# Attention, value copies and unit outputs in another order, one query chunk in a second bank

## The chip, the cores and the metric

The kernel runs on one core of a Trainium2 chip. The metric is the device time of one execution in microseconds (us); the number compared is the median of several executions. TensorE is called PE here, VectorE DVE, ScalarE ACT, GpSimd POOL, as in the profile.

## The reference

The model is one block of four phases on x, 1024 tokens by 256 features, each phase added to x behind a layer norm: attention, a mixture-of-experts feed-forward network, a state-space mixer, and the same feed-forward network again. The change is in the attention alone:

```python
q = (x @ wq.T).reshape(b, t, 16, 128).transpose(0, 2, 1, 3)      # 16 heads of 128
k = (x @ wk.T).reshape(b, t, 4, 128).transpose(0, 2, 1, 3)       # 4 key/value heads, each for 4 query heads
v = (x @ wv.T).reshape(b, t, 4, 128).transpose(0, 2, 1, 3)
scores = einsum('bhtd,bhsd->bhts', q, k_full) / sqrt(128)
mask = (k <= q) & ((k < 4) | (k >= q - 31))                       # 4 sink keys and a window of 32
attn = masked softmax of scores in float32
x = x + einsum('bhts,bhsd->bhtd', attn, v_full).reshape(b, t, 2048) @ wo.T
```

## The kernel before, in words

**Numbers.** Most products work on a high and a low part of each float32 operand (`three`, line 164: high by high, high by low, low by high), so a result that feeds another product is written twice: ACT copies the high part out of PSUM, then DVE subtracts it from the same PSUM bank and writes the low part. The bank is free only when the low part is out.

**Tiles.** The attention goes over 4 groups g (a key/value head with its 4 query heads), and in each over NJ = 11 units j: the first has 128 tokens, the others 90 (the last overlaps the one in front). That makes NU = 44 units. A unit is scores (PE), mask and row maximum (DVE, `row_max`), exponentials with their sums (ACT, `exps`, 4 pieces of 128x128 in a first unit and 3 pieces of 120x66 in the others, each an activation and an accumulator read), reciprocal of the sums (DVE, `recip`), normalisation (POOL, `normalise`), transposes (PE, `p_transpose`), high and low parts of the transposed probabilities (`pT_hi` L598 on ACT, `pT_lo` L691 on DVE), product with the values (PE, `p_v`), and high and low parts of the output (`oT_hi` L607 on ACT, `oT_lo` L697 on DVE).

**The value stage.** Ahead of the main loop a loop over j (lines 472, 581 and 676 for PE, ACT and DVE) makes the values of the 11 units. PE alternates between banks 4 and 5: value product j waits until low part j - 2 is out (`s_vlo`). ACT makes the high part (L585), DVE the low part (L680). The first three units are started inside this loop: `FIRST_UNITS` puts the scores, maxima and exponentials of units 0, 1 and 2 at j = 5, 7 and 9, and on ACT and DVE they stand in front of the value copy of the same j; `RECIPS` puts the reciprocals of units 0 and 1 behind j = 6 and 8.

**The main loop** (lines 526, 609 and 706) has one step i for each unit and some behind the last, 50 in all (0 to 49). Each engine has a fixed order within a step and runs its own list; only semaphores tie them together. In step i:

- PE: scores(i), query chunks of the step, projection of an output tile, p_v(i - 4), p_transpose(i - 2).
- ACT: copies of the query chunks (`q_evac`, L566), pT_hi(i - 3), oT_hi(i - 5), exps(i), and the high part of a weight in some steps.
- DVE: row_max(i), recip(i - 1), pT_lo(i - 3), the residual add of the step's tile (`add`, L704), in the last group the layer-norm statistics of that tile (L207, L210), oT_lo(i - 5), and in steps 44 to 48 the first stages of the next phase.
- POOL: gathers of keys, normalise(i - 1), low parts of weights.

A query chunk is 6 matmuls into bank 6 (`queries`, line 438); ACT copies it to `qT`, and the next chunk waits for that copy. Chunks 0 to 3 are in the value stage, chunks 4, 5 and then 6 and 7 together in steps 2, 3 and 4; units whose tokens lie behind 512 (from unit 5 on) wait for all eight. A projection (`project`, line 515) is 12 matmuls into bank 7. It waits for the low part of the last unit that its tile needs, which is oT_lo(i - 6), of the step before, and for the add that empties bank 7. p_v(i - 4) writes the bank of unit i - 6 (banks 4 and 5 in turn), so it too waits for oT_lo(i - 6). Each of the 8 tiles of a group has its projection in the step that lies 6 behind the last unit it needs: in the last group these are steps 39, 41, 42, 44, 45, 47, 48 and 49.

**The seam.** The next phase's stages for the first half of the tokens are queued into the last steps: on DVE `veps0` (step 44, L214), `norm0` (step 45, four L227), `lo0` (46), `logits_copy0` (47), `split0` (48, two low parts of weights, L867), on POOL `rstd0` (L221), on PE `tr0` (step 46, transposes, L235), `logits0` (47), `logits_tr0` (48), and then products of the next phase.

The DVE order of a step before the change:

```python
if 0 <= i - LAG_P < NU:
    pT_lo(i - LAG_P)
if i in y_tile:
    add(y_tile[i])
    if y_tile[i] >= (KV - 1) * NT:
        early(phase, "stats", e, y_tile[i] % NT)
if 0 <= i - LAG_F < NU:
    oT_lo(i - LAG_F)
```

Of the kernel before, what the change touches and what calls it, by code (L numbers as in the profile page):

```python
# [26 lines left out]
ACT = mybir.ActivationFunctionType  # L27
# [7 lines left out]
HALF = T // 2  # L35
# [7 lines left out]
HEADS, KV, HD = 16, 4, 128  # L43
GROUP = HEADS // KV
SINK, WINDOW = 4, 32
QB, NB_Q = 30, 3
# [8 lines left out]
NJ = 1 + -(-(T - P) // QT_LEN)  # L55
# [45 lines left out]
def build(nc, ins, out, phases=4):  # L101
    ctx = ExitStack()
    with ctx:
# [51 lines left out]
        def bank(i):  # L155
            return PS[:, i, :]
# [7 lines left out]
        def three(e, dst, lhs, rhs, start, stop, **kw):  # L164

            for n, (a, b) in enumerate(TERMS):
                i = e.matmul(dst, lhs(a), rhs(b), start=start and n == 0,  # L167
                             stop=stop and n == len(TERMS) - 1, **kw)
            return i
# [93 lines left out]
        def early(phase, stage, e, *args):  # L263

            if stage in phase["next"]:
                phase["next"][stage](e, *args)


        def attention():
# [3 lines left out]
            wq_hl = at("wq_hl", [P, 2, 2, KB, HALF], F32R, A_W)  # L273
            raw = at("w_raw", [P, 4, 1024], F32, A_W + 16384)
            qT = at("qT", [P, T, GROUP], F32, A_Q)
# [15 lines left out]
            s_q, s_qt, s_mask = sem("q_mm"), sem("q_ev"), sem("masked")  # L291
# [7 lines left out]
            phase = {"next": {}}  # L299
            units = [(g, j) for g in range(KV) for j in range(NJ)]  # L300
            NU = len(units)
# [13 lines left out]

            LAG_T, LAG_P, LAG_O, LAG_F, LAG_Y = 2, 3, 4, 5, 6
            FIRST_UNITS = {NJ - 6: 0, NJ - 4: 1, NJ - 2: 2}
            RECIPS = {NJ - 5: 0, NJ - 3: 1}
            NF = len(FIRST_UNITS)
            q_chunk = {NF - 1 + i: [GROUP + i] for i in range(3)}  # L320
            q_chunk[NF + 1].append(2 * GROUP - 1)
# [84 lines left out]
            def pe(e):  # L406
# [31 lines left out]
                def queries(n):  # L438
                    g, h = n // (2 * GROUP), n % GROUP
                    half = n // GROUP % 2  # L440
                    e.wait_ge(s_wl, WQ[g])
                    if n:
                        e.wait_ge(s_qt, n)
                    for k in range(KB):
                        m = three(e, bank(6), lambda w: wq_hl[:, g % 2, w, k, h * HD:(h + 1) * HD],
                                  lambda w: xT[:, w, k, HALF * half:HALF * half + HALF], k == 0, k == KB - 1)
                    m.then_inc(s_q, 1)

# [66 lines left out]
                def project(n):  # L515
                    g, t = n // NT, n % NT
                    e.wait_ge(s_olo, g * NJ + last_unit[t] + 1)
                    e.wait_ge(s_wl, WO[g])
                    if n:
                        e.wait_ge(s_add, n)  # L520
                    for h in range(GROUP):
                        m = three(e, bank(7)[:, 0:D], lambda w: oT_hl[:, w, h, t * P:(t + 1) * P],
                                  lambda w: wo_hl[:, g % 2, w, h, :], h == 0, h == GROUP - 1)
                    m.then_inc(s_y, 1)
# [21 lines left out]
            def act(e):  # L546
                ln["hi"](e, 0)
                w_hi(e, 0)
                w_hi(e, 1)
                w_hi(e, 2)  # L550
                ln["hi"](e, 1)
                e.wait_ge(LN["hi"], 2 * KB)
                for k in range(KB):
                    gather(e, lambda o, i: e.activation(o, i, ACT.Copy), HI, k).then_inc(s_xg, 1)
                ln["ready"](e)
                for k in range(KB):
                    gather(e, lambda o, i: e.activation(o, i, ACT.Copy), LO, k).then_inc(s_xg, 1)

                def q_evac(n):
                    h, half, g = n % GROUP, n // GROUP % 2, n // (2 * GROUP)  # L560
                    e.wait_ge(s_q, n + 1)
                    if g and half == 0:
                        e.wait_ge(s_s, (g - 1) * NJ + 6)
                    if g and half == 1:
                        e.wait_ge(s_s, g * NJ)
                    e.activation(qT[:, HALF * half:HALF * half + HALF, h], bank(6), ACT.Copy,  # L566
                                 scale=float(HD) ** -0.5).then_inc(s_qt, 1)

                def exps(u):
                    e.wait_ge(s_max, u + 1)  # L570
                    if u >= 4:
                        e.wait_ge(s_rd, u - 3)
                    rows, parts, p = probs(u)
                    for n in range(parts):
                        m = e.activation(p[:, n, :], p[:, n, :], ACT.Exp, bias=NEGM[0:rows, u % 4, n:n + 1],  # L575
                                         accum_out=DEN[0:rows, u % 4, n:n + 1])
                    m.then_inc(s_exp, 1)

                w_hi(e, 3)
                w_hi(e, 4)  # L580
                for j in range(NJ):
                    if j in FIRST_UNITS:
                        exps(FIRST_UNITS[j])
                    e.wait_ge(s_v, j + 1)
                    e.activation(v_hl[0:NK[j], HI, j, :], bank(4 + j % 2)[0:NK[j], :], ACT.Copy).then_inc(s_vhi, 1)  # L585
                    if j < GROUP:
                        q_evac(j)
                e.wait_ge(s_par, 16)
                e.wait_ge(s_cf, 16)
                e.activation(gw_hl[:, GW_PARTS:], cf[:, 0:GW_PAD - GW_PARTS], ACT.Copy, scale=0.0)  # L590
                e.activation(gw_hl[:, 0:GW_PARTS // 2], par[:, PR_GW:PR_CS], ACT.Copy).then_inc(s_gwh, 1)

                def pT_hi(u):
                    n, nk = GROUP * QN[units[u][1]], NK[units[u][1]]
                    e.wait_ge(s_t, u + 1)
                    if u >= 2:
                        e.wait_ge(s_o, u - 1)
                    e.activation(pT_hl[0:nk, u % 2, HI, 0:n], bank(2 + u % 2)[0:nk, 0:n], ACT.Copy).then_inc(s_phi, 1)  # L598

                def oT_hi(u):  # L600
                    g, j = units[u]
                    e.wait_ge(s_o, u + 1)
                    if g:
                        e.wait_ge(s_y, (g - 1) * NT + min(NT, -(-(Q0[j] + QN[j]) // P)))
                    if j and Q0[j] < Q0[j - 1] + QN[j - 1]:
                        e.wait_ge(s_olo, u)
                    e.activation(out_view(oT_hl[:, HI], j), out_psum(u, j), ACT.Copy).then_inc(s_ohi, 1)  # L607

                for i in range(STEPS):
                    for n in q_chunk.get(i, ()):  # L610
                        q_evac(n)
                    if 0 <= i - LAG_P < NU:
                        pT_hi(i - LAG_P)
                    if 0 <= i - LAG_F < NU:
                        oT_hi(i - LAG_F)
                    if NF <= i < NU:
                        exps(i)
                    if i in w_step:
                        w_hi(e, w_step[i])
                    if i == NU + 2:  # L620
                        early(phase, "hi0", e)

            def dve(e):
# [64 lines left out]
                def pT_lo(u):  # L688
                    n, nk = GROUP * QN[units[u][1]], NK[units[u][1]]
                    e.wait_ge(s_phi, u + 1)  # L690
                    e.tensor_tensor(pT_hl[0:nk, u % 2, LO, 0:n], bank(2 + u % 2)[0:nk, 0:n],  # L691
                                    f32(pT_hl[0:nk, u % 2, HI, 0:n]), ALU.subtract).then_inc(s_plo, 1)

                def oT_lo(u):
                    g, j = units[u]
                    e.wait_ge(s_ohi, u + 1)
                    e.tensor_tensor(out_view(oT_hl[:, LO], j), out_psum(u, j), f32(out_view(oT_hl[:, HI], j)),  # L697
                                    ALU.subtract).then_inc(s_olo, 1)
# [7 lines left out]
                for i in range(STEPS):  # L706
                    if NF <= i < NU:
                        row_max(i)
                    if NF <= i < NU + 1:
                        recip(i - 1)  # L710
                    if 0 <= i - LAG_P < NU:
                        pT_lo(i - LAG_P)
                    if i in y_tile:
                        add(y_tile[i])
                        if y_tile[i] >= (KV - 1) * NT:
                            early(phase, "stats", e, y_tile[i] % NT)
                    if 0 <= i - LAG_F < NU:
                        oT_lo(i - LAG_F)
                    for step, stage in ((NU, "veps0"), (NU + 1, "norm0"), (NU + 2, "lo0"), (NU + 3, "logits_copy0"),
                                        (NU + 4, "split0")):  # L720
                        if i == step:
                            early(phase, stage, e)

# [1419 lines left out]
```

## Time and profile before

| | |
|---|---|
| median of 3 runs | 570.72 us (568.29 to 571.48) |
| profiled execution, its own time | 568.28 us |
| its span, first to last instruction | 566.5 us |
| PE busy (matmul / weight load) | 525.1 us (93%) / 441.1 us (78%) |
| DVE, ACT, POOL busy | 405.4, 307.6, 127.2 us |
| granted TensorE clock | 0.995 |

The attention takes roughly the first 214 us of the span: layer norm and keys until about 26 us, the value stage until about 52, the main loop until about 214, of which the part behind the last scores (steps 44 to 49) begins at about 197. A busy PE in the profile is not yet PE at its peak, since matmuls overlap and their ends are modelled. An idle time in brackets is that of the row's engine ahead of the row, with what ended it.

### The profile page before, as it was taken

The numbers are of one execution on the slowest core, as the hardware profiler recorded it, in microseconds if no ns is written. First come the engines' busy times: TensorE is split into PE (matmuls) and PEld (weight loads), VectorE is DVE, ScalarE is ACT, GpSimd is POOL, SyncE is SP. The second block draws the span as 40 slices with busy tenths as digits, with TensorE's granted clock in tenths as the row PEclk, the third lists the DMA queues.
The fourth block names the chain that finished last, engine by engine and source line by source line (L and its number), as shares of the span: only waits on it lengthen the run. The fifth ranks groups of instructions, "written<-read, shape, count | busy, mean of one in ns | idle before, by whom it ended". The sixth has DMA issues, their size and how long they took to land.

```text
span 566.5 us, 9078 instructions
## 1 busy us (share of the span) xinstructions
PE 525.1 (93%) x3047; PEld 441.1 (78%) x3049; DVE 405.4 (72%) x895; ACT 307.6 (54%) x758; POOL 127.2 (22%) x272
## 2 busy tenths in 40 slices
PE   6998899999999888799999999999899889999994
PEld 4777799998999877577887887757777668788883
DVE  6534565666566878799877888957876868877684
ACT  3655778688677742454342455888752244333341
POOL 2322324244243210000000004667542000000000
PEclk9999999999999999999999999999999999999998
DMA  7320100000004003000030000000000000000101
GB/s 264 109 75 1 38 2 2 2 1 1 2 2 144 2 1 135 1 1 1 0 131 0 1 2 0 1 1 1 2 0 2 1 0 2 0 2 0 38 1 38
DMA packets 5790, 14.25 MB, mean 25 GB/s; under 512 B 624, under 2 KB 2928, under 8 KB 5744
## 3 DMA queue, kind: packets, MB, share of 16 engines
q1 hardware_dynamic: 5744, 13.66, 6.9%
q8 instruction: 25, 0.41, 0.3%
q14 instruction: 21, 0.17, 0.1%
HBM read 12.61 MB, written 1.05 MB: 24 GB/s over the span
## 4 chain that ended last, share of the span: by engine, by line
PE 65%; DVE 19%; ACT 7%; issue 6%; POOL 1%; DMA 1%; DVEq 0%; ACTq 0%; POOLq 0%
PE psum L167 53%; PE psum L468 2%; DVE f_t L1203 2%; DVE f_um L1213 2%; DVE oT_hl L697 1%; PE psum L500 1%; PE psum L235 1%; DVE ln_stats L207 1%; DVE x_resid L704 1%; ACT qT L566 1%; PE psum L997 1%; ACT pT_hl L598 1%; DVE xT_hl L249 1%; ACT f_sil L1110 1%; PE psum L1611 1%
## 5 line engine op out<-in xcount | busy, mean ns | idle before, releaser
L167 PE MATMUL psum<-xT_hl,ffn_w_hl 128*128 128x512 f32 x312 | 78.1, 397 | 7.3 <-DVE f_t L1203 7.3
L167 PE MATMUL psum<-f_um,ffn_w_hl 128*128 128x512 f32 x288 | 72.1, 398 | 1.2 <-DVE f_um L1213 1.2
L167 PEld LDWEIGHTS psum<-xT_hl,ffn_w_hl 128*128 128x128 f32 x312 | 56.3, 188 | 19.6 <-issue 8.7
L167 PEld LDWEIGHTS psum<-f_um,ffn_w_hl 128*128 128x128 f32 x288 | 53.5, 188 | 14.3 <-DVE f_um L1213 2.1
L1203 DVE TENSOR_TENSOR f_t<-psum,f_sil 128x512 f32<-128x512 f32 (+1 forms) x48 | 33.2, 691 | 32.8 <-ACT f_sil L1110 32.2
L1110 ACT ACTIVATE f_sil<-psum 128x512 f32<-128x512 f32 (+1 forms) x48 | 28.3, 597 | 51.8 <-PE psum L167 51.8
L167 PE MATMUL psum<-wo_hl,oT_hl 128*128 128x256 f32 x384 | 50.9, 282 | 4.1 <-DVE oT_hl L697 4.0
L691 DVE TENSOR_TENSOR pT_hl<-psum,pT_hl 126x360 fp32r<-126x360 f32 (+1 forms) x44 | 23.6, 537 | 42.9 <-ACT pT_hl L598 42.9
L167 PE MATMUL psum<-xT_hl,wq_hl 128*128 128x512 f32 x192 | 52.3, 407 | 1.9 <-ACT qT L566 1.9
L167 PEld LDWEIGHTS psum<-wo_hl,oT_hl 128*128 128x128 f32 x384 | 47.7, 188 | 7.5 <-DVE oT_hl L697 5.8
L1131 ACT ACTIVATE f_ch_hl<-f_ch 128x512 fp32r<-128x512 f32 x48 | 30.1, 630 | 41.4 <-DVE f_ch L1260 41.3
L566 ACT ACTIVATE qT<-psum 128x512 f32<-128x512 f32 x32 | 35.0, 1094 | 31.3 <-PE psum L167 31.3
L575 ACT ACTIVATE probs<-probs,small 120x66 f32<-120x66 f32 x120 | 40.8, 348 | 7.8 <-DVE small L674 7.1
L167 PEld LDWEIGHTS psum<-xT_hl,wq_hl 128*128 128x128 f32 x192 | 33.8, 189 | 9.2 <-issue 3.4
L167 PE MATMUL psum<-f_ch_hl,ffn_w_hl 128*128 128x512 f32 x144 | 37.8, 398 | 1.4 <-DVE f_ch_hl L1272 1.4
L167 PEld LDWEIGHTS psum<-ffn_w_hl,f_mix_hl 128*128 128x128 f32 x288 | 36.9, 188 | 2.8 <-DVE x_resid L1294 0.8
L167 PE MATMUL psum<-ffn_w_hl,f_mix_hl 128*128 128x256 f32 x288 | 37.7, 280 | 0.0
L746 POOL TENSOR_TENSOR probs_wide<-probs,small 120x186 f32<-120x186 f32 x40 | 20.0, 500 | 69.6 <-DVE small L654 69.3
L1260 DVE TENSOR_TENSOR f_ch<-f_t,f_wb 128x512 f32<-128x512 f32 x48 | 33.2, 691 | 1.4
L221 POOL TENSOR_TENSOR ln_rstd<-ln_var_eps,minus_half 128x4 f32<-128x4 f32 x8 | 8.1, 1012 | 114.5 <-DVE ln_var_eps L214 114.5
L167 PEld LDWEIGHTS psum<-f_ch_hl,ffn_w_hl 128*128 128x128 f32 x144 | 26.6, 188 | 8.7 <-DVE f_ch_hl L1272 2.0
L167 PE MATMUL psum<-pT_hl,v_hl 126*128 126x360 f32 (+1 forms) x132 | 30.5, 339 | 1.1 <-DVE oT_hl L697 0.6
(238 smaller groups left out, 1128.6 us busy)
## 6 DMA issues: line engine op xcount, KB each, us to landing
w_raw<-in_wq SPq DMA_DIRECT2D x4, 512.0 KB, 3.9
w_raw<-in_wo SPq DMA_DIRECT2D x4, 512.0 KB, 3.3
ffn_w_raw<-in_ffn SPq DMA_DIRECT2D x3, 576.0 KB, 6.3
ffn_w_raw_far<-in_ffn SPq DMA_DIRECT2D x3, 576.0 KB, 5.1
ssd_w_raw<-in_ssd SPq DMA_DIRECT2D x3, 512.0 KB, 5.4
x_resid<-in_x SPq DMA_DIRECT2D x2, 512.0 KB, 4.6
out_x<-x_resid SPq DMA_DIRECT2D x4, 256.0 KB, 2.3
w_raw<-in_wk SPq DMA_DIRECT2D x1, 512.0 KB, 6.6
```

The source lines that it names most:

```text
L167: i = e.matmul(dst, lhs(a), rhs(b), start=start and n == 0, stop=stop and n == len(TERMS) - 1, **kw)
L221: e.tensor_tensor(rstd[:, seg], veps[:, seg], minus_half[:, seg], ALU.pow).then_inc(LN["rstd"], 1)
L468: m = e.matmul(bank(u % 2)[0:ROWS, i * KBLK:(i + 1) * KBLK], queries_of(q, QB), kw[:, w % W_SLOTS, i, :], start=True, stop=True)
L566: e.activation(qT[:, HALF * half:HALF * half + HALF, h], bank(6), ACT.Copy, scale=float(HD) ** -0.5).then_inc(s_qt, 1)
L575: m = e.activation(p[:, n, :], p[:, n, :], ACT.Exp, bias=NEGM[0:rows, u % 4, n:n + 1], accum_out=DEN[0:rows, u % 4, n:n + 1])
L691: e.tensor_tensor(pT_hl[0:nk, u % 2, LO, 0:n], bank(2 + u % 2)[0:nk, 0:n], f32(pT_hl[0:nk, u % 2, HI, 0:n]), ALU.subtract).then_inc(s_plo, 1)
L746: e.tensor_tensor(wide, p[:, :, SINK:KBLK], spread(r, KB_WIN), ALU.mult)
L1110: e.activation(sil[at_rows, s, :], bank(i % 2)[rows, :], ACT.Silu).then_inc(FS[f"sil{s}"], 1)
L1131: e.activation(ch_hl[:, i % 2, s, HI, :], ch[:, i % 2, s, :], ACT.Copy).then_inc(FS["chh"], 1)
L1203: e.tensor_tensor(tt[rows, s, :], to_bank(i, 1)[rows, :], sil[rows, s, :], ALU.mult).then_inc(FS[f"t{s}"], 1)
L1213: e.tensor_tensor(um_hl[:, h, s, which, w, :], f32(us_hl[:, h, which, w, :]), mT[:, (0, 2)[s], half(h)], ALU.mult).then_inc(FS["um"], 1)
L1260: e.tensor_tensor(ch[:, i % 2, s, :], tt[:, s, :], wb[:, s, half(h)], ALU.mult).then_inc(FS[f"ch{s}"], 1)
```

## The change

Four edits, all within `attention()`.

- Value stage, ACT: the value copy of step j now stands in front of the exponentials, and unit 0's four exponential pieces are split, two behind value copy 5 and two behind value copy 6 (`EXPS`; `exps` takes the pieces as an argument and signals behind the last one). The exponentials of units 1 and 2 stay at j = 7 and 9, behind the copy.
- Value stage, DVE: the reciprocals of units 0 and 1 stand behind low parts 7 and 9 instead of 6 and 8.
- Query chunk 7 (`Q_PAIR`) goes into bank 7 and does not wait for the copy of chunk 6. The projections, which use bank 7, wait for its copy.
- Main loop, DVE: oT_lo(i - 5) stands in front of the add and the statistics; `norm0` (step 45) stands between the two.

```diff
-            RECIPS = {NJ - 5: 0, NJ - 3: 1}
+            RECIPS = {NJ - 4: 0, NJ - 2: 1}
+            EXPS = {NJ - 6: (0, (0, 1)), NJ - 5: (0, (2, 3)), NJ - 4: (1, range(NB_Q)), NJ - 2: (2, range(NB_Q))}
+            Q_PAIR = 2 * GROUP - 1
...
-                    if n:
+                    if n and n != Q_PAIR:
                         e.wait_ge(s_qt, n)
                     for k in range(KB):
-                        m = three(e, bank(6), lambda w: wq_hl[:, g % 2, w, k, h * HD:(h + 1) * HD],
+                        m = three(e, bank(7 if n == Q_PAIR else 6), lambda w: wq_hl[:, g % 2, w, k, h * HD:(h + 1) * HD],
...
                     e.wait_ge(s_wl, WO[g])
+                    e.wait_ge(s_qt, Q_PAIR + 1)
...
-                def exps(u):
+                def exps(u, some=None):
...
-                    for n in range(parts):
+                    for n in range(parts) if some is None else some:
...
-                    m.then_inc(s_exp, 1)
+                    if n == parts - 1:
+                        m.then_inc(s_exp, 1)
...
                 for j in range(NJ):
-                    if j in FIRST_UNITS:
-                        exps(FIRST_UNITS[j])
                     e.wait_ge(s_v, j + 1)
                     e.activation(v_hl[0:NK[j], HI, j, :], bank(4 + j % 2)[0:NK[j], :], ACT.Copy).then_inc(s_vhi, 1)
                     if j < GROUP:
                         q_evac(j)
+                    if j in EXPS:
+                        exps(*EXPS[j])
...
                         pT_lo(i - LAG_P)
+                    if 0 <= i - LAG_F < NU:
+                        oT_lo(i - LAG_F)
+                    if i == NU + 1:
+                        early(phase, "norm0", e)
                     if i in y_tile:
                         add(y_tile[i])
                         if y_tile[i] >= (KV - 1) * NT:
                             early(phase, "stats", e, y_tile[i] % NT)
-                    if 0 <= i - LAG_F < NU:
-                        oT_lo(i - LAG_F)
-                    for step, stage in ((NU, "veps0"), (NU + 1, "norm0"), (NU + 2, "lo0"), (NU + 3, "logits_copy0"),
-                                        (NU + 4, "split0")):
+                    for step, stage in ((NU, "veps0"), (NU + 2, "lo0"), (NU + 3, "logits_copy0"), (NU + 4, "split0")):
```

## Rows read from the trace of the kernel before

**Rows 1.** Busy time of each engine in three stretches, core 0

```profile
core 0: us, PE busy (x) PEld busy (x) DVE busy (x) ACT busy (x) POOL busy (x), PEclk, DMA share, GB/s
39.00:64.00 25.00, 21.36 (x113) 17.21 (x113) 10.88 (x29) 14.70 (x46) 4.29 (x13) 1.00 0.00 1
64.00:185.00 121.00, 119.57 (x854) 110.73 (x855) 76.46 (x229) 92.60 (x311) 48.95 (x134) 1.00 0.07 23
185.00:214.00 29.00, 24.10 (x179) 21.67 (x178) 23.83 (x71) 15.73 (x51) 5.83 (x17) 1.00 0.00 1
```

**Rows 2.** Waits of PE in 39 to 64 us: us in total, times, longest

```profile
PE psum L167 <- ACT qT L566: 1.9, 3, 1.3
PE psum L167 <- DVE v_hl L680: 1.6, 2, 1.3
```

**Rows 3.** Waits of PE in 185 to 214 us

```profile
PE psum L167 <- DVE oT_hl L697: 3.6, 6, 1.3
PE psum L235 <- DVE xn L227: 1.2, 1, 1.2
```

**Rows 4.** Timeline of the value stage: start, us, engine, what, [idle before it]

```profile
39.87 3.03 PE L167 MATMUL psum<-wv_hl,xg_hl 128*126 128x512 f32 x12
...
41.84 0.41 ACT L575 ACTIVATE probs_first<-probs_first,small 128x128 f32<-128x128 f32 x1 [2.08 <-DVE small L674]
...
43.41 1.06 ACT L585 ACTIVATE v_hl<-psum 126x512 fp32r<-126x512 f32 x2
44.02 1.29 DVE L680 TENSOR_TENSOR v_hl<-psum,v_hl 126x512 fp32r<-126x512 f32 x2 [2.21 <-ACT v_hl L585]
...
44.76 3.04 PE L167 MATMUL psum<-wv_hl,xg_hl 128*126 128x512 f32 x12 [1.28 <-DVE v_hl L680]
```

**Rows 5.** Timeline around the last two query chunks of the first group

```profile
57.24 1.64 PE L167 MATMUL psum<-xT_hl,wq_hl 128*128 128x512 f32 x6 [0.36 <-ACT qT L566]
...
60.14 1.64 PE L167 MATMUL psum<-xT_hl,wq_hl 128*128 128x512 f32 x6 [1.26 <-ACT qT L566]
...
61.81 1.09 ACT L566 ACTIVATE qT<-psum 128x512 f32<-128x512 f32 x1 [1.82 <-PE psum L167]
...
63.00 0.81 PE L468 MATMUL psum<-k_windows,qT 128*120 128x66 f32 x6 [0.22 <-issue]
```

**Rows 6.** Waits of PE in 64 to 185 us

```profile
PE psum L167 <- DVE oT_hl L697: 1.0, 3, 0.3
```

**Rows 7.** Timeline of a middle step with a projection (add and low part of step 9, product of step 10)

```profile
80.35 0.41 DVE L704 TENSOR_TENSOR x_resid<-psum,x_resid 128x256 f32<-128x256 f32 x1
...
80.68 0.52 DVE L697 TENSOR_TENSOR oT_hl<-psum,oT_hl 128x360 fp32r<-128x360 f32 x1
...
81.32 0.47 PEld L167 LDWEIGHTS psum<-pT_hl,v_hl 126*128 126x128 f32 x3 [0.25 <-issue]
```

**Rows 8.** Timeline of the last steps (42 to 49)

```profile
192.74 1.65 PE L167 MATMUL psum<-wo_hl,oT_hl 128*128 128x256 f32 x12 [0.22 <-DVE oT_hl L697]
...
197.82 1.68 PE L167 MATMUL psum<-wo_hl,oT_hl 128*128 128x256 f32 x12 [0.67 <-DVE oT_hl L697]
...
199.54 0.42 DVE L704 TENSOR_TENSOR x_resid<-psum,x_resid 128x256 f32<-128x256 f32 x1 [0.85 <-PE psum L167]
...
200.56 0.50 DVE L697 TENSOR_TENSOR oT_hl<-psum,oT_hl 128x360 fp32r<-128x360 f32 x1
...
201.11 1.66 PE L167 MATMUL psum<-wo_hl,oT_hl 128*128 128x256 f32 x12 [0.80 <-DVE oT_hl L697]
201.28 1.01 POOL L221 TENSOR_TENSOR ln_rstd<-ln_var_eps,minus_half 128x4 f32<-128x4 f32 x1 [2.35 <-DVE ln_var_eps L214]
...
204.24 1.38 DVE L227 TENSOR_SCALAR xn<-x_resid,ln_mean_var,ln_rstd 128x256 f32<-128x256 f32 x4
...
213.10 1.68 PE L167 MATMUL psum<-wo_hl,oT_hl 128*128 128x256 f32 x12 [1.27 <-DVE oT_hl L697]
...
214.82 0.42 DVE L704 TENSOR_TENSOR x_resid<-psum,x_resid 128x256 f32<-128x256 f32 x1
```

More of the change, by code:

```diff
@@ L565, in q_evac @@
                         e.wait_ge(s_s, g * NJ)
-                    e.activation(qT[:, HALF * half:HALF * half + HALF, h], bank(6), ACT.Copy,
+                    e.activation(qT[:, HALF * half:HALF * half + HALF, h], bank(7 if n == Q_PAIR else 6), ACT.Copy,
                                  scale=float(HD) ** -0.5).then_inc(s_qt, 1)
-                def exps(u):
+                def exps(u, some=None):
                     e.wait_ge(s_max, u + 1)
```

## The prediction

> **What bounds the kernel now.** I read the page first: PE is busy for 93% of the span, so a change pays only where it takes idle time from PE or from what stands behind PE's next work. Then I cut the part that the diff touches into three stretches and asked for the busy time of each engine [rows 1]. Between 64 and 185 us PE idles for 1.4 us of 121: a PE-bound stretch in which an earlier DVE can give almost nothing. In the value stage (39 to 64) PE idles for 3.6 us of 25, in the last steps (185 to 214) for 4.9 of 29, and there DVE is nearly as busy as PE (23.8 against 24.1). Next, PE's waits. In the value stage they are 1.6 us for value low parts and 1.9 us for copies of query chunks [rows 2], in the last steps 3.6 us for oT_lo and 1.2 us for the normalised x of the next phase [rows 3]. These are the waits at which the four edits aim, 8.3 us in all, and the ceiling short of a knock-on. The timelines [rows 4, 5, 7, 8] say which of it can go.
>
> **Edit 1, value copies ahead of the first exponentials (with the later reciprocals).** Value products 5 and 6 run from 39.87 to 42.9, so product 5 is complete at about 41.4. ACT could copy it then, but stands in front of exps(0), waiting for the maximum until 41.84, and comes to the copy only at 43.41; the low part starts at 44.02 and product 7 at 44.76, after 1.28 us of PE idle time [rows 4]. In the new order the copy runs from 41.4 to 42.0 (two take 1.06), and the low part (two take 1.29) is out at about 42.7, before PE is free at 44.76 - 1.28 = 43.5. The 1.28 us go. The same holds for product 9, whose wait is what is left of the 1.6 us, 0.3 [rows 2, 4]. Sum 1.5 us. Nothing is added to any engine; the pieces of exps(0) are only split around copy 6. What is later: reciprocals 0 and 1, by about 1 us. Their users are the transposes of steps 2 and 3, behind four more value products (3 us in rows 4 for two), so that is covered; without that cover it would cost the 1 us.
>
> **Edit 2, chunk 7 in bank 7.** Chunk 6 starts at 57.24 and chunk 7 at 60.14, after 1.26 us of idle time for the copy of chunk 6. The copy of chunk 7 (61.81, 1.09 us) ends at 62.9 and scores(5), which needs all eight chunks, starts at 63.00 [rows 5]. Without the wait chunk 7 starts at 58.9, its copy at 60.55 (ACT is free of copy 6 by 60.1), scores(5) at 61.7: 1.3 us earlier. The product of unit 0 and a transpose that ran beside the copy still run beside it. The other two waits for copies (0.36 in rows 5 and 0.3) stay. Projections gain a wait for copy 7; the first comes at step 6, long behind, and costs nothing. Edits 1 and 2 are in series: 2.8 us earlier into the main loop. The weight split that ACT and POOL do in step 4 moves with it. No DMA is added or moved past another in SP's list; those that wait for a semaphore of this phase start as much earlier as it.
>
> **Edit 3, oT_lo ahead of the add, in the middle.** The bound needs care. A projection in the next step waits for both oT_lo and the add, so swapping these (0.52 and 0.41 us) leaves the later of them where it was: the three waits of 0.33 us [rows 6] stay. Where the next step has no projection, only p_v waits, and only for oT_lo: the add starts at 80.35, oT_lo at 80.68, p_v loads at 81.32 after 0.25 us [rows 7]. Swapped, oT_lo is out 0.33 us earlier and the gap closes. It occurs three times (here, at 120.9 and at 160.6), so 0.75 us. Bounds: nothing, and the 1.4 us of all idle time of this stretch [rows 1]; I take 0.75.
>
> **Edit 4, the same in the last steps, and norm0 moved.** Here the add is followed by statistics, so oT_lo starts 1.02 us behind the add's start (199.54 and 200.56) and the projection at 201.11 waits for it [rows 8]. Walked step by step:
> - Steps 39 to 43: DVE itself is full, its work per step is as long as PE's, so part of the waits only moves from one cause to another. I get 0.4 us at 197.82 (the wait of 0.22 at 192.74 and as much again in front of DVE's next mask). Bounds 0 and 1.7, the waits before 201.
> - Steps 44 and 45: DVE sat idle for 0.85 us in front of the add; oT_lo fits into that. The add then ends 2.14 us behind the start of its projection, and PE is through with its own work at 201.11 - 0.80. Gain 0.8 to 1.0, together 1.3.
> - norm0: the variance is ready about 0.9 us sooner, POOL's power (201.28, 1.01 us) ends at about 201.45, and norm0 no longer stands behind an add, its statistics and oT_lo: it starts at 201.5 instead of 204.24, 2.7 us sooner, and tr0 with it.
> - Steps 46 to 49: the add and statistics of step 45 now lie behind norm0's 1.38 us, so pT_lo(43), oT_lo(41) and lo0 gain only 1.6. From there the swap gains again, since oT_lo(43) no longer waits behind an add and statistics: the last projection (213.10, waited 1.27) comes at about 210.35, 2.75 sooner, and the last add (214.82) only 2.0 sooner, since two weight low parts (split0) stand in front of it on DVE.
>
> Behind this seam PE runs without a break for some 7 us, so the gain handed on is nearer to PE's: I take 2.5 of 2.0 to 2.75. DVE is busy there too, and that is the reason not to take it all.
>
> **Sum.** 2.8 + 0.75 + 2.5 = 6.05, say 6.0 us of the profiled execution: 568.3 - 6.0 = 562.3 (its span 566.5 to 560.5). That execution lies 2.4 us under the median of the three runs and at their lowest, so the median forecast is 570.7 - 6.0 = **564.7 us**, 1.05% less. About 0.5% (2.85 us) is what a measurement of this kernel tells from no change.
>
> **A page against the rows.** Between 64 and 185 us the weight-load column shows 110.7 us of 121 where the matmul column shows 119.6 [rows 1]. In the same stretch the view of waits finds a single cause, 1.0 us [rows 6]. Six loads of a chunk take less than its matmuls, so loads can leave holes while PE streams; I keep 1.4 us as the ceiling of the middle. The Trainium skill (Perfetto Trace Analysis, Identifying the Most-Contended Engine) says that matmul busy time is no good measure of TensorE's headroom and that the share of weight loads should be used. By that measure the middle would have 10.3 us of headroom, not 1.4, and the swap could win several us more there. The trace speaks for it only in the column, not in any wait.
>
> **The rivals.**
> - **A, the forecast** (gain 4.5 to 7.5): chance 0.70.
> - **B, DVE bounds the seam.** With 23.8 us of 29 [rows 1] DVE cannot hand on what PE wins; norm0 in front of an add that two later steps need gives back what it takes. The seam then gives 0.4 to 1, the sum is 2.8 + 0.75 + 0.7 = 4.2, time 566.5. For it: oT_lo(41) gains 1.1 less than tr0 in my walk. Against: DVE's idle time there, 0.85 in front of one add alone. 0.12.
> - **C, the value stage gives nothing.** The diff would not do what it says if the maximum or POOL's gathers bind the first units, so that an earlier product 7 only waits longer for the next thing; the same where the next phase swallows the shift. Then the seam alone remains, 2.5 or less: 568.2 to 570.7, say 569. Against it: no other wait than those two stands in [rows 2]. 0.10.
> - **D, slower: the add holds bank 7.** The add is now up to 0.5 us later in every step, and bank 7 is single. If PE reached the next projection before the add's end in each of the 19 places where projections stand in neighbouring steps, that is 9.5 us against 6.0 won: 570.7 + 3.5 = 574.2. It decides from the point where oT_lo is not needed by that projection anyway; by the step lags it always is (oT_lo(i - 5) is the unit of the projection in step i + 1), so only oT_hi being late could make it so, and in rows 7 both DVE operations ran back to back. 0.04.
> - **E, the middle has headroom** as the weight-load column would have it: the 0.33 us of rows 7 at all nine places where a step without a projection follows one with it, 3 us in place of 0.75, gives 562.5 with the rest as forecast and 561.7 with the whole seam. Against it [rows 6]. 0.04.
>
> **How the numbers follow.** The likeliest case gives 564.7. Its own spread (4.5 to 7.5 gained) gives 563.2 to 566.2; three runs before spread over 3.2 us, so I widen by 1.3 below, to 561.8 (which also takes in E in part), and above to B and the better half of C: 568.8. Left out are D, most of C, some of E: under 0.2. Faster by over 0.5%: A, E and two thirds of B, 0.82. Within 0.5%: C and the rest of B, 0.14. Slower: 0.04.
>
> **What the profile after would show.** Right if: product 7 of the value stage starts at about 43.5 without a wait; chunk 7 follows chunk 6 by about 1.5 us in place of 2.9, and scores(5) stand at about 60.2; the span from scores(5) to the end of step 38 is unchanged within 1 us; norm0 starts about 6 us before its 204.24; DVE's idle time in front of the adds is gone. Step 1 is wrong if PE waits at a first transpose; edit 3 if x_resid L704 shows up as what ends PE's idle time in the middle; edit 4 if PE's waits for oT_lo between its last scores and last projection are replaced by as long waits for the add. The forecast fails as a whole if the phases behind 214 us begin 6 us sooner and end less than 4 sooner.

## The result, and the profile after

The changed kernel took 561.25 us (median of 4, 561.13 to 561.34), the kernel before 569.5 us beside it (median of 4, 568.15 to 571.48): 8.25 us less, ratio 0.9852, interval 0.9816 to 0.9888. The forecast was 564.7 us with a range down to 561.8, so the change gained more than forecast and than the range held. The profiled execution took 561.34 us at a span of 559.6, against 568.28 and 566.5: between the two profiles the gain is 6.9 us, where the sum said 6.05.

Busy time by stretch, cut at about the same work as [rows 1]:

```profile
core 0: us, PE busy (x) PEld busy (x) DVE busy (x) ACT busy (x) POOL busy (x), PEclk, DMA share, GB/s
39.00:61.00 22.00, 21.17 (x116) 17.60 (x116) 11.65 (x30) 15.10 (x48) 4.28 (x13) 1.00 0.00 1
61.00:181.50 120.50, 119.23 (x859) 110.93 (x858) 76.19 (x232) 91.99 (x311) 48.81 (x134) 1.00 0.07 23
181.50:208.00 26.50, 23.46 (x179) 21.62 (x178) 23.46 (x67) 15.35 (x51) 5.83 (x17) 1.00 0.01 2
```

PE's idle time fell from 3.6 to 0.8 us in the value stage and from 4.9 to 3.0 in the last steps; the middle kept its share. PE's waits in the same three stretches, in this order (five rows against [rows 2, 3, 6]):

```profile
PE psum L167 <- ACT qT L569: 0.6, 2, 0.4
...
PE psum L167 <- DVE x_resid L708: 1.3, 3, 0.4
...
PE psum L167 <- DVE oT_hl L701: 2.6, 3, 1.1
PE psum L167 <- DVE x_resid L708: 0.3, 1, 0.3
PE psum L235 <- DVE xn L227: 0.2, 1, 0.2
```

The waits for value low parts are gone and one of three for query copies. In the middle the same three waits stand, now for the add instead of oT_lo, a little longer (1.3 for 1.0): the swap only changes which of the two comes last, as the forecast had it. The timeline, value stage and query chunks ([rows 4, 5]), then the last steps ([rows 8]); lines that do not bear on the argument are left out (`...`):

```profile
39.84 3.03 PE L167 MATMUL psum<-wv_hl,xg_hl 128*126 128x512 f32 x12
...
41.51 0.60 ACT L587 ACTIVATE v_hl<-psum 126x512 fp32r<-126x512 f32 x1 [1.77 <-PE psum L167]
...
43.26 3.02 PE L167 MATMUL psum<-wv_hl,xg_hl 128*126 128x512 f32 x12
...
55.26 3.03 PE L167 MATMUL psum<-xT_hl,wq_hl 128*128 128x512 f32 x12 [0.36 <-ACT qT L569]
...
59.52 0.81 PE L470 MATMUL psum<-k_windows,qT 128*120 128x66 f32 x6 [0.22 <-issue]
...
180.15 1.62 PE L167 MATMUL psum<-wo_hl,oT_hl 128*128 128x256 f32 x12
...
193.08 1.65 PE L167 MATMUL psum<-wo_hl,oT_hl 128*128 128x256 f32 x12 [1.13 <-DVE oT_hl L701]
...
195.34 1.62 PE L167 MATMUL psum<-wo_hl,oT_hl 128*128 128x256 f32 x12
...
196.22 1.01 POOL L221 TENSOR_TENSOR ln_rstd<-ln_var_eps,minus_half 128x4 f32<-128x4 f32 x1 [2.04 <-DVE ln_var_eps L214]
...
197.37 1.38 DVE L227 TENSOR_SCALAR xn<-x_resid,ln_mean_var,ln_rstd 128x256 f32<-128x256 f32 x4 [0.31 <-POOL ln_rstd L221]
...
200.67 1.65 PE L167 MATMUL psum<-wo_hl,oT_hl 128*128 128x256 f32 x12 [0.94 <-DVE oT_hl L701]
...
206.24 1.62 PE L167 MATMUL psum<-wo_hl,oT_hl 128*128 128x256 f32 x12 [0.27 <-DVE x_resid L708]
```

Product 7 starts at 43.26 with no wait, chunks 6 and 7 run as one piece (the row at 55.26), scores(5) start at 59.52, 3.5 us earlier than at 63.00. Of the last steps one row more of before is needed, the projection of step 39:

```profile
184.43 1.62 PE L167 MATMUL psum<-wo_hl,oT_hl 128*128 128x256 f32 x12
```

So I can cut both traces at three points that do not depend on when an execution started: from value product 5 to scores(5) (value stage and chunks), from there to the projection of step 39 (middle), from there to the last projection (last steps), and from there to the end of the span.

| us | to scores(5) | middle | last steps | to the end |
|---|---|---|---|---|
| before | 23.13 | 121.43 | 28.67 | 353.4 |
| changed | 19.68 | 120.63 | 26.09 | 353.4 |
| gain, and as forecast | 3.45 (2.8) | 0.80 (0.75) | 2.58 (2.5) | 0.0 |

The three gains add to 6.8 us and are handed to the end whole. Two things are left to explain: the forecast's first column is 0.65 us too small, and the gain of the profiles (6.9 us) lies 1.3 us under that of the medians (8.25).

### The profile page after: what moved, and what is told of

The parts are those of the page before. It is cut to its first block, busy times and chain, and to the rows that moved or that the text cites. A ratio compares the mean times of both kernels' runs of the same rounds, so it can differ in the third digit from the quotient of the medians.

```text
span 559.6 us, 9110 instructions
## 1 busy us (share of the span) xinstructions
PE 523.0 (93%) x3049; PEld 441.0 (79%) x3049; DVE 405.3 (72%) x895; ACT 306.6 (55%) x758; POOL 126.9 (23%) x272
## 4 chain that ended last, share of the span: by engine, by line
PE 71%; DVE 16%; issue 5%; ACT 5%; POOL 2%; DMA 1%; DVEq 0%; ACTq 0%; POOLq 0%
PE psum L167 58%; PE psum L470 4%; DVE f_t L1208 2%; DVE f_um L1218 2%; PE psum L502 2%; PE psum L235 1%; PE psum L1002 1%; DVE xT_hl L249 1%; DVE ln_stats L207 1%; ACT f_sil L1115 1%; PE psum L1616 1%; PE psum L463 1%; DVE f_hot L1184 1%; PE psum L1620 1%; PE psum L412 1%
## 5 line engine op out<-in xcount | busy, mean ns | idle before, releaser
L1277 DVE TENSOR_TENSOR f_ch_hl<-f_ch,f_ch_hl 128x512 fp32r<-128x512 f32 x48 | 30.9, 686 | 0.0
```

Of the source, the lines that this page charges most:

```text
L1277: e.tensor_tensor(ch_hl[:, i % 2, s, LO, :], ch[:, i % 2, s, :], f32(ch_hl[:, i % 2, s, HI, :]), ALU.subtract).then_inc(FS["chl"], 1)
```

## The experiments

**Edit 1 alone (e1), edit 2 alone (e2), edits 3 and 4 alone (e3), edits 1 and 2 (e7).** Each is the kernel before with a part of the diff above: e1 without `Q_PAIR` and with DVE's loop as before; e2 only the `Q_PAIR` lines; e3 only DVE's loop; e7 all but DVE's loop.

> Edit 1 alone on the kernel before (value copies ahead of the first exponentials, reciprocals 0 and 1 one value product later); chunk 7 stays in bank 6, DVE's main loop as before. Theory S (the forecast's mechanism, with sizes taken from start to start instead of from the idle time in brackets): product 7 of the value stage 1.5 us earlier, product 9 another 0.5, scores(5) 2.0 us earlier, span 2.0 under the 566.5 of before. Rival F (the forecast's own size): 1.5. Rival I (the edits only pay together, since the earlier query chunks meet the same copies): under 1.

> Edit 2 alone on the kernel before (query chunk 7 in bank 7). Theory S: chunk 7 starts 1.5 us behind chunk 6 instead of 2.9, scores(5) and the span 1.5 earlier (565.0). Rival F: 1.3. Rival I: under 0.7.

> Edits 3 and 4 alone on the kernel before (unit output low part ahead of the add in every step, normalisation of the next phase ahead of the add of step 45). Theory S: scores(5) where they were, 0.8 us earlier at the first scores of step 39, 3.4 us at the last projection, span 563.1. Rival F: 3.25, span 563.25. Rival I (the last steps gain only when the loop comes to them earlier): under 2.

> Edits 1 and 2 together, DVE's main loop as before. By e1 and e2 scores(5) come 3.5 us earlier (59.5 instead of 63.0), the undisturbed span is 563.0 and the undisturbed time 564.8. Rival L (part of it is lost on the way through the loop, so that edits 3 and 4 gain 3.4 on either base but these two less): scores(5) at 59.5 and the last projection less than 3.3 us earlier than 213.1.

Measured, with the same cuts (ratio to the kernel before on the same chip; e1, e2 and e3 ran beside a median of 571.0 and a lowest of 568.4 us, e7 beside 568.59 and 567.97):

| | to scores(5) | middle | last steps | to the end | median, lowest (executions) | ratio, interval |
|---|---|---|---|---|---|---|
| e1 | 21.20 | 121.33 | 28.58 | 354.5 | 569.75, 566.96 (10) | 0.9981, 0.9958 to 1.0003 |
| e2 | 21.61 | 121.60 | 28.66 | 354.6 | 568.37, 567.96 (10) | 0.9984, 0.9959 to 1.0008 |
| e3 | 23.10 | 120.61 | 26.08 | 353.6 | 565.0, 564.78 (4) | 0.9906, 0.9879 to 0.9933 |
| e7 | 19.69 | 121.56 | 28.66 | 353.6 | 565.13, 564.72 (9) | 0.9945, 0.9922 to 0.9968 |

Up to the last projection theory S holds to a tenth: 1.93 and 1.52 us add to e7's 3.44, e3's 0.8 and 2.6 are those of the whole change, and e3 and e7 together make the whole (lowest executions against the lowest of the kernel before beside them: 3.6 and 3.3 of 7.0). Rival I, that the edits only pay together, falls, and so does rival L, that the loop swallows a part (e7 keeps 3.3 of its 3.44 us up to the last projection). But e1 and e2, at the last projection 2.1 and 1.4 us ahead when counted from value product 5, end only 1.4 and 0.0 ahead in their profiles, and the intervals of both ratios hold 1. The stretch to the end tells why: it is 1.1 and 1.2 us longer than before. Behind 236 us of e2, in the first feed-forward phase:

```profile
core 0: us, PE busy (x) PEld busy (x) DVE busy (x) ACT busy (x) POOL busy (x), PEclk, DMA share, GB/s
236.00:238.00 2.00, 1.68 (x16) 1.49 (x14) 0.18 (x1) 0.88 (x2) 0.00 (x0) 1.00 0.00 0
238.00:239.00 1.00, 0.00 (x0) 0.00 (x0) 0.16 (x1) 1.00 (x3) 0.00 (x0) 1.00 0.00 0
239.00:240.00 1.00, 0.32 (x2) 0.31 (x3) 1.00 (x2) 1.00 (x2) 0.00 (x0) 1.00 0.00 0
240.00:241.00 1.00, 1.00 (x5) 0.82 (x4) 1.00 (x3) 0.35 (x1) 0.00 (x0) 0.80 0.00 0
241.00:242.00 1.00, 1.00 (x3) 0.72 (x3) 1.00 (x3) 0.00 (x0) 0.00 (x0) 0.50 0.00 0
242.00:243.00 1.00, 1.00 (x4) 0.79 (x3) 0.90 (x2) 0.00 (x0) 0.00 (x0) 0.50 0.00 0
243.00:244.00 1.00, 1.00 (x4) 0.52 (x2) 0.92 (x2) 0.00 (x0) 0.00 (x0) 0.50 0.00 0
244.00:246.00 2.00, 2.00 (x22) 1.91 (x22) 0.85 (x2) 1.48 (x3) 0.00 (x0) 1.00 0.00 0
```

PEclk is the granted clock: 0.50 (1.2 of 2.4 GHz) for some 3.5 us, behind a pause of PE that ends at 239.68. The twelve matmuls behind it take 4.57 us there (first row), and 3.00 in the changed kernel (second row), where the same pause stands and the clock does not fall:

```profile
239.68 4.57 PE L167 MATMUL psum<-xT_hl,ffn_w_hl 128*128 128x512 f32 x12 [1.99 <-DVE f_t L1205]
```

```profile
233.97 3.00 PE L167 MATMUL psum<-xT_hl,ffn_w_hl 128*128 128x512 f32 x12 [1.99 <-DVE f_t L1208]
```

e1 has the same drop at 239 us. (The last 5 us or so of the span show 0.50 in nearly every profile; they are not counted as a drop.) The times of the kernel before point to it too: they are not spread evenly but lie at 567.8 to 569.1 us (the lower level, called undisturbed here) or at 570.3 us and more (the upper level), and the mean granted clock of an execution is 0.994 to 0.996 at the lower level (0.992 or 0.993 in five executions at its upper edge) and 0.986 to 0.994 at the upper.

**Both kernels again (e5, e6).** No edit.

> The changed kernel unchanged, for more executions. What is asked: whether its single level of 561.1 to 561.3 us is a property of it or chance. The kernel before has two levels, 568.4 to 568.6 at a granted clock of 0.995 and 571.0 to 571.7 at 0.988 to 0.994. Theory C (the two levels are a drop of TensorE's clock somewhere in the later phases, which the change moves but does not remove): of the executions some show 0.993 or less and 563.5 to 564.5 us, the others 561.2. Rival P (the change removes it): all within 0.4 us of 561.2.

> The kernel before unchanged, for a profile beside more executions. Theory C: executions at 568.5 and at 571 us, about half and half; if the profiled one is of the upper level, its trace shows a stretch behind 214 us at a clock below 1.00 other than the last 10 us, with matmuls about twice as long, and the attention (first 214 us) as in the lower level. Rival Q (the upper level comes from the attention, a late transfer or a wait in it): the attention is 2 us longer in it.

The changed kernel has the upper level too: three executions at 561.38, 561.52 and 561.68 and three at 564.13, 564.23 and 564.39. So the result's four executions at 561.1 to 561.3 were all of the lower level by luck, or by the chip that they ran on; over all ten the median is 561.45. The profiled one of e5 was an upper one (564.39). Its attention is as long as in the first profile (19.69, 120.62 and 26.03 in the three cuts), but the last stretch takes 356.7 instead of 353.4, with drops of the clock at 427 us, in the mixer, and at 457 us, behind the same pause in the second feed-forward phase. The first:

```profile
core 0: us, PE busy (x) PEld busy (x) DVE busy (x) ACT busy (x) POOL busy (x), PEclk, DMA share, GB/s
425.00:427.00 2.00, 2.00 (x19) 2.00 (x19) 1.57 (x5) 0.05 (x1) 0.32 (x1) 1.00 0.00 0
427.00:429.00 2.00, 2.00 (x8) 1.61 (x7) 1.13 (x4) 0.00 (x0) 0.68 (x2) 0.52 0.00 0
429.00:431.00 2.00, 2.00 (x7) 1.60 (x6) 1.01 (x2) 0.00 (x0) 0.10 (x1) 0.62 0.00 0
```

The pause itself, with the twelve matmuls behind it, stands twice in this one execution, without a drop in the first feed-forward phase and with one in the second:

```profile
233.70 3.00 PE L167 MATMUL psum<-xT_hl,ffn_w_hl 128*128 128x512 f32 x12 [1.99 <-DVE f_t L1208]
...
456.98 4.58 PE L167 MATMUL psum<-xT_hl,ffn_w_hl 128*128 128x512 f32 x12 [1.99 <-DVE f_t L1208]
```

e6 ran six times at 567.93 to 568.92 and four times at 570.88 to 571.45; its profile was a lower one, so rival Q is answered only by e5's, for the changed kernel. No profile of the kernel before at its upper level exists. Over all 124 executions of the kernel before in this study 60 lie above 570 us, 13 of them even above 572.8, a third level.

**The pause filled (e9 on the changed kernel, e11 on the kernel before).**

```diff
                 weigh(0)
+                need(e, "wbc", 1)
+                for _ in range(5):
+                    e.matmul(bank(6)[:, 0:2 * P], ident, cf[:, 0:2 * P], start=True, stop=True)
```

> The changed kernel with five matmuls into a free bank in each of the two feed-forward phases, where PE stood idle for 2.0 us in front of a product that waits for f_t (at 231.98 us of the changed kernel's profile); their result is not used. Theory G (the granted clock falls to one half behind this pause in part of the executions, and that is the upper level): fewer executions at 563.5 and above, undisturbed ones at 561.2 to 561.5. Theory H (the drop comes at other pauses too, so this pause is one of several places): the share stays near one in three and the drop is found elsewhere. Rival W (the added matmuls cost more than they save): all executions 0.5 us or more above 561.4.

> The kernel before with the same five matmuls in the same pause of both feed-forward phases. Theory G: the upper level of 571 us becomes rarer than the two in five seen for the kernel before, the median falls to 568.4. Theory H: about as often as before. Rival W: the lower level rises to 569 or more.

Where PE stood idle for 2.0 us, e9 shows the added matmuls (ten passes, 2.38 us) and goes on without a wait:

```profile
231.42 2.38 PE L1026 MATMUL psum<-const_f 128*128 128x256 f32 x10
```

e11: 568.06 us, twelve executions within 567.85 to 568.88, none at 571, while nine of 17 of the unfilled kernel before on the same chip were at 570.3 or more (median 570.31). e9: 561.47, six within 561.25 to 562.06. Theory G holds for these two kernels: with this pause filled in both feed-forward phases the level of 3 us more is gone. The profiles agree. Without the fill, each of the five profiled executions with two drops (e4, e5, e10, e12, e18) had one behind this pause in the second feed-forward phase, at 457 to 462 us, and e10 and e18 another in the first; with the fill no profile has a drop at either place. With the pause filled the change is worth 568.06 - 561.47 = 6.6 us by medians, 6.6 by the lowest. H is right in small: e9's profile still has a drop at 426 us, in the mixer, and took 562.06.

**Does the place in time decide (e17, e18)?** The changed kernel with 16 or 11 idle matmuls ahead of the value stage.

```diff
                         e.wait_ge(s_kev, KV)
+                        keep_busy(16)    # e18: 11
```

> The changed kernel with 16 matmuls of 128x256 ahead of the value stage (0.307 us each by the 12 of the start, 4.9 us), their result unused: all behind is 4.9 us later, 2.1 us earlier than in the kernel before, as in e1. Theory T (the place in time decides): nearly all executions have a drop, time 561.3 + 4.9 = 566.2 only as the floor, most at 567 to 570. Rival Z (chance, the same for every kernel): two in three at 566.2 to 566.5.

> The same with 11 matmuls (3.4 us): 3.6 us earlier than the kernel before, as e3 and e7. Theory T: a drop in about one execution of three, the others at 564.7 to 565.0, median 564.9. Rival Z: the same share; if e17's share is as this one's, theory T falls.

The delays came out larger than I had written, 7.1 and 4.9 us: e17's trace shows the 16 as 32 passes in 7.07 us and e18's the 11 as 22 in 4.91, so a float32 matmul of this form runs as two, and the 12 of the start that I had read were six. So e17 stands about where the kernel before stands (last projection at 213.44 against 213.10 us) and e18 where e1 stands (210.71 against 210.59). Read so: of twelve executions e17 had five at 568.33 to 568.55, one at 569.13 and six at 570.96 or more, the kernel before beside it twelve at 568.07 to 568.51 and eleven at 570.77 or more; e18 had one of twelve at 565.62 and eleven at 567.35 to 570.39, as e1, which had none of ten at its undisturbed 566.4. Taken by the places that I had named the expectations fail; taken by the places that the runs had, the share of drops fits the place in time and not the edits. This is a reading behind the fact, and not shown: it is two places only, e1 ran on another chip than e18, and a place is known to no better than about 1 us, since the same work ahead of value product 5 ends anywhere between 39.4 and 40.9 us in the profiles. What the place has to coincide with is open.

**e1, e2, e3 with the pause filled (e13, e14, e15).**

> e1 (edit 1 alone) with the pause of the feed-forward phases filled. To be compared with e11 (kernel before, pause filled: 568.06 median, 567.85 lowest). Theory S: 2.0 us less, median 566.1. Rival F: 1.5, 566.6. Rival I: under 1, over 567.1.

> e2 (edit 2 alone) with the pause filled, compared with e11. Theory S: 1.5 us less, median 566.6. Rival F: 1.3, 566.8. Rival I: under 0.7.

> e3 (edits 3 and 4 alone) with the pause filled, compared with e11. Theory S: 3.4 us less, median 564.7; with e13 and e14 the sum is 6.9, as e9 against e11 in their lowest executions (6.6).

e15 came out as said (565.14, 565.04 to 566.09, ten executions; 2.9 us under e11 by medians and 2.8 by the lowest, or 3.1 if one allows that the kernel before was 0.3 us slower on e15's chip, of 3.4 expected). e13 and e14 did not: medians 567.94 and 568.51, twelve executions each, though the lowest were 565.5 and 565.68. Filling one pause was not enough at these places: the profiled execution of each shows a mean clock of about 0.7 between 430 and 435 us, in the mixer, and 354.4 and 354.5 us to the end, 1.1 and 1.2 more than e11's 353.3. So the first two columns stand by their starts (e1, e2) and by e7. In the median edit 1 alone was worth 0.1 us against e11 and edit 2 alone was 0.45 us slower than e11, on another chip. That each moves the program to a bad place in time is the likely reason, not a shown one.

**Parts of the last steps (e4, e8, e12, e10, e16).** e4 puts norm0 behind the add again; e8 puts the statistics of step 45 behind oT_lo(41); e10 does both; e16 is e10 with the pause filled; e12 puts the two reciprocals back.

```diff
e10:
-                    if i == NU + 1:
-                        early(phase, "norm0", e)
+                    if i == NU + 2:
+                        early(phase, "stats", e, y_tile[NU + 1] % NT)
                     if i in y_tile:
                         add(y_tile[i])
-                        if y_tile[i] >= (KV - 1) * NT:
+                        if y_tile[i] >= (KV - 1) * NT and i != NU + 1:
...
+                    for step, stage in ((NU, "veps0"), (NU + 1, "norm0"), (NU + 2, "lo0"), ...
```

> The changed kernel with the normalisation of the next phase behind the add and its statistics again (the swap itself stays). Forecast's walk: the normalisation starts about 1.0 us later than in the changed kernel (an add and statistics in front), the transposes with it; pT_lo(43) and oT_lo(41) are not later, since DVE does the same work, so the last projection is 0 to 0.5 us later and the span at 559.6 to 560.1. Rival N (the move of the normalisation is what wins the last steps): 2 us later, 561.6. Rival D (the normalisation ahead of the add costs): the span falls by 0.3 or more.

> The changed kernel with the statistics of tile 4 (step 45) behind oT_lo(41) (step 46) on DVE. In the changed kernel PE waits 0.94 us at 200.67 for oT_lo(41), behind an add and 0.57 us of statistics. If DVE bounds these steps: that projection 0.5 us earlier, the last projection 0.2 to 0.5 earlier, undisturbed time 560.8 to 561.0. Rival (the next stage lo0 needs DVE at the same time and passes the loss on): last projection where it was, 561.2.

> The changed kernel with the reciprocals of units 0 and 1 behind low parts 6 and 8 again. The forecast took their move as free either way (covered by 3 us): undisturbed 561.2, scores(5) within 0.1 us of where they are counted from product 5. If they stood in front of DVE's low part 7 or row maximum 1 at a bad moment: product 9 or 10 up to 0.4 us later, scores(5) and the time 0.4 later.

> The changed kernel with two moves in the last steps on DVE: the normalisation of the next phase behind the add of step 45 again, and the statistics of that step's tile behind oT_lo(41) of step 46. From the last projection of e4 (0.3 us earlier against the changed kernel) and e8 (0.55 earlier): if they add, last projection 0.85 us earlier counted from scores(5), undisturbed time 560.3. Rival (both take the same idle time of DVE): 0.55, 560.6.

> e10 (normalisation behind the add again, statistics of step 45 behind the next unit output) with the pause filled. In e10's trace the last projection comes 1.1 us earlier, counted from scores(5), than in the changed kernel. If that reaches the end: 1.0 us under e9 (561.47 median, 561.25 lowest), median 560.4, faster than both kernels. Rival: the next phase gives back half of it, 561.0; or it brings the drop of the clock nearer (as in e10), 561.5 or more.

| | last steps | time, lowest to highest (executions) |
|---|---|---|
| changed, e5 | 26.09, 26.03 | 561.13 to 564.39 (10) |
| e12 | 26.00 | 561.22 to 564.2 (4) |
| e4 | 25.80 | 560.86 to 564.09 (4) |
| e8 | 25.47 | 560.33 to 565.25 (5) |
| e10 | 25.00 | 561.63 to 564.49 (6) |
| e16 | 25.10 | 559.9 to 560.34 (6) |

The reciprocals are free either way (e12: 19.69 to scores(5)). norm0 ahead of the add does not win; it costs 0.25 to 0.3 us (e4, rival D of that run). In e8 the wait of step 47 shrinks from 0.94 to 0.28 us:

```profile
199.77 1.68 PE L167 MATMUL psum<-wo_hl,oT_hl 128*128 128x256 f32 x12 [0.28 <-DVE oT_hl L701]
```

The two add up in the trace (1.0 to 1.1 us against the changed kernel), yet e10's six executions all had a granted clock of 0.992 or less and its median, 562.44, is no better than the changed kernel's. With the pause filled the gain arrives: **e16 takes 560.02 us**, six executions within 0.45 us, ratio 0.9817 (0.977 to 0.9863) to the kernel before, 1.45 us under e9, which ran on another chip. It beats both kernels.

## Why the prediction was right or wrong

The mechanism of all four edits was right; the forecast of 564.7 us was 3.45 us too high by two steps. One is the last step of the sum, which added 2.4 us for the distance of the profile to the median; the other is the size of the terms for edits 1 and 2, 0.65 us short. The rest, 0.4 us, is rounding and small differences.

- **Edit 1: mechanism right, size short.** "The 1.28 us go", and 0.3 with product 9, sum 1.5; e1 shows 1.93. Product 7 moved from 44.76 to 43.26 (1.50), product 9 by 0.5. The idle time in brackets is counted from the modelled end of the last matmul, while the next product can start before that end: each removed wait gives back the distance between starts, 0.2 us more than its bracket. In the changed kernel the scores ahead of product 7 end at 42.71 + 0.74 = 43.45 by the model and product 7 starts at 43.26. The reciprocals were covered, as said (e12).
- **Edit 2: the same step failed the same way.** 1.3 forecast from the bracket of 1.26; e2 shows 1.52, the distance from start to start less the work. These two terms are 0.65 of the 0.9 us by which the sum was short.
- **Edit 3: the place right, the size by luck.** 0.75 forecast, 0.8 measured in every kernel with the swap (120.6 against 121.4). But it is not three times 0.25. At the first of the three places ([rows 7]), from the start of the scores of step 10 to the start of its product with the values, it took 0.89 us before (first two rows) and 0.55 in the changed kernel (last two), 0.34 less, again more than the bracket of 0.25:

```profile
80.46 0.75 PE L468 MATMUL psum<-k_windows,qT 128*120 128x66 f32 x6
81.35 0.74 PE L167 MATMUL psum<-pT_hl,v_hl 126*128 126x360 f32 x3
...
76.98 0.75 PE L470 MATMUL psum<-k_windows,qT 128*120 128x66 f32 x6
77.53 0.74 PE L167 MATMUL psum<-pT_hl,v_hl 126*128 126x360 f32 x3
```

  The three waits of steps with neighbouring projections, now for the add, are each 0.1 us longer and take 0.3 us back, where the forecast had them unchanged. Rival E falls: the weight-load column stands at 110.9 of 120.5 us as before, and yet only 0.8 us came. The Trainium skill (Perfetto Trace Analysis, Identifying the Most-Contended Engine) judges TensorE's headroom by that column and by the matmul work done per time; for what a change of order could win here, the view of waits was the better measure. E's time with the whole seam, 561.7, does not follow from its own terms either: 2.8 + 3 + 2.75 gives 562.15.
- **Edit 4: sum right (2.58 for 2.5), one step wrong.** Counted from the projection of step 39, that of step 44 came 0.46 us earlier (193.08 - 180.15 against 197.82 - 184.43), that of step 45 1.5, norm0 2.6 and the last projection 2.6, where the walk had 0.4, 1.3, 2.7 and 2.75. But the walk credited norm0's own move with the gain. e4 shows that the swap makes it: with norm0 behind the add again, norm0 starts 0.7 us later and the last projection is 0.3 sooner, since DVE waits 0.31 us for POOL's power anyway (196.22, 197.37) and most of the add's 0.42 us fits there. "The gain handed on is nearer to PE's": all of it was, 353.4 us to the end in both, so rivals B and C fall.
- **Rival D falls** by the rows of the middle: the add became what PE waits for in exactly the three places where oT_lo had been, 0.1 us longer each.
- **The 2.4 us between profile and median was the step that failed most.** I carried the distance of the profiled execution to the median (570.7 - 568.3) over to the changed kernel as if it were a property of the measurement. The runs show in its place a second level, 2.5 to 3 us higher, in about one of two executions (60 of 124), that is gone when the pause is filled (e11, none of twelve) and that in e5's profile is a drop of TensorE's clock. The forecast for an undisturbed execution was 568.3 - 6.0 = 562.3, 1.0 us from the 561.34 measured; with the 2.4 it was 564.7. The changed kernel's first four executions had none of the upper level, which is why the measured gain is 8.25 us. Between the lowest executions it is 7.0. Had they shared out like e5's, the median would have lain nearer to the forecast: e5's own is 562.91.

## What to carry to other kernels

Size a removed wait from start to start of the work on both sides of it, not from its idle time: the bracket was 0.1 to 0.3 us short each time here. Look at the spread of the times before forecasting: here levels with different granted clocks meant that a pause far behind the change decided the median, and gains of 1.5 and 1.9 us in the attention (e2, e1) could not be told from nothing by the times. Fill or remove such a pause first (here five idle matmuls), then judge small edits, and look for further pauses: at e13's and e14's places one fill was not enough.

## What the runs showed of the hardware that was not expected

A pause of PE of 2.0 us, between stretches in which it was busy, is followed in part of the cases by a granted clock of 0.50 for some 3.5 us, and in the others not. Both stand in one execution of e5: twelve matmuls took 3.00 us behind the first such pause and 4.58 behind the second. Whole executions of one kernel on one chip differ in the same way (e5: 561.38 us at a mean clock of 0.996, 564.39 at 0.989).

How often it happened differed with the kernel, and by the times fits the place of the pause in time: about one in two for the kernel before and for the changed kernel moved back by 7.1 us (e17), nearly always 1.2 to 2.5 us ahead of that (e1, e2, e18, by their last projections), three of ten for the changed kernel. Against a rule as simple as that stand e8 and e10, whose last steps are only 0.6 and 1.1 us shorter: four of five and six of six. The chips differ too.

In the profiles one drop cost 1.1 to 1.2 us (e1, e2, e13, e14), two together 2.9 to 3.5 (e10, e5, e18), counted from the last projection to the end, against 353.4 us. The drop in the mixer at 426 to 432 us stands behind shorter pauses, 1.0 us the longest of the 20 us ahead of it in e5, and was not filled. What the place has to coincide with stays open.
